# Softmax row sums by VectorE block transposes, with the sums' last merge taken from GpSimd, in an attention and mixture-of-experts layer

## What is computed

```python
h = _layernorm(x) * (1 + ca) + sa
xq, xk, xv = h @ wq.T, h @ wk.T, h @ wv.T        # each reshaped to (heads, 2048, 64)
scores = softmax(einsum('bhid,bhjd->bhij', xq, xk) * SCALE, axis=-1)
out = einsum('bhij,bhjd->bhid', scores, xv)
x = x + ga * (out.reshape(bsz, seqlen, 1024) @ wo.T)
h = _layernorm(x) * (1 + cb) + sb
x = x + gb * ffn(h)                              # routed experts and a shared one
```

## Time and profile before

| | |
|---|---|
| median of 3 runs | 1318.63 us (1318.17 to 1810.67) |
| the profiled execution | 1317.36 us |
| its span, first to last instruction | 1315.6 us |
| PE busy | 1297.5 us, 99% of the span |
| POOL busy | 1176.0 us, 89% |
| DVE busy | 911.3 us, 69% |
| ACT busy | 888.3 us, 68% |
| mean granted TensorE clock | 0.999 of full speed |

### The profile page before, as it was taken

How to read it: one execution, slowest core, us unless ns; L and a number is a source line. 1 busy time by engine, 2 the same in 40 slices (tenths; PEclk the granted TensorE clock), 3 DMA queues, 4 the chain that set the end, 5 groups by cost and what they waited for, 6 DMA issues and landing times. The chain is left out here.

```text
span 1315.6 us, 22284 instructions
## 1 busy us (share of the span) xinstructions
PE 1297.5 (99%) x8792; PEld 705.3 (54%) x8792; DVE 911.3 (69%) x1036; ACT 888.3 (68%) x1096; POOL 1176.0 (89%) x538
## 2 busy tenths in 40 slices
PE   7999999999999999999999999999999999999998
PEld 5545545454555545454555555454545545454787
DVE  6767667676767677677767676776767676859575
ACT  6666767676766766666766666676767667775474
POOL 2499999999999999999999999999999999999644
PEclk9999999999999999999999999999999999999999
DMA  8010202020110202020100202020200102001323
GB/s 210 11 39 1 49 1 49 1 49 1 27 24 1 49 1 49 1 49 1 38 13 1 49 1 49 2 49 0 49 1 10 40 1 49 1 1 30 101 73 89
DMA packets 31962, 41.55 MB, mean 32 GB/s; under 512 B 4298, under 2 KB 15186, under 8 KB 31858
## 3 DMA queue, kind: packets, MB, share of 16 engines
q1 hardware_dynamic: 31714, 40.13, 12.5%
q10 hardware_dynamic: 144, 0.00, 0.0%
HBM read 13.70 MB, written 1.11 MB: 11 GB/s over the span
## 5 line engine op out<-in xcount | busy, mean ns | idle before, releaser
L918 ACT ACTIVATE probs<-ps 128x1024 f32<-128x1024 f32 x512 | 498.7, 1032 | 78.7 <-PE ps L1348 75.9
L1079 DVE TENSOR_REDUCE peak_parts<-ps 128x2 f32<-128x1024 f32 x297 | 362.2, 1223 | 236.8 <-PE ps L1289 235.1
L1366 PE MATMUL ps<-probs,v_sb 128*64 128x512 f32 x2048 | 522.8, 606 | 0.0
L1009 POOL TENSOR_TENSOR acc<-acc,probs 128x1024 f32<-128x1024 f32 x192 | 457.7, 2384 | 31.2 <-ACT probs L918 29.6
L1009 POOL TENSOR_TENSOR acc_odd<-acc_odd,probs 128x1024 f32<-128x1024 f32 x192 | 459.5, 2393 | 0.0
L860 ACT COPY peak_copy<-ps 128x1024 f32<-128x1024 f32 x215 | 218.6, 1017 | 242.0 <-PE ps L1289 168.0
L1089 DVE TENSOR_REDUCE peak_parts<-peak_copy 128x2 f32<-128x1024 f32 x215 | 260.7, 1212 | 34.2 <-ACT peak_copy L860 34.2
L1366 PEld LDWEIGHTS ps<-probs,v_sb 128*64 128x64 f32 x2048 | 123.8, 136 | 157.3 <-issue 118.4
L1342 PE MATMUL ps<-q_hi,d_swap_hi 64*128 64x512 f32 x512 | 201.4, 393 | 0.4 <-ACT probs L918 0.4
L1342 PE MATMUL ps<-q_hi,d_hi 64*128 64x512 f32 x512 | 201.5, 394 | 0.0
L1348 PE MATMUL ps<-q_hi,d_swap_lo 64*128 64x512 f32 x512 | 200.7, 392 | 0.0
(11 more groups left out here) (237 smaller groups left out, 1571.6 us busy)
## 6 DMA issues: line engine op xcount, KB each, us to landing
k_swap_hi<-k_hi SPq DMA_DIRECT2D x64, 128.0 KB, 2.3
d_swap_hi<-d_hi SPq DMA_DIRECT2D x64, 128.0 KB, 2.3
d_swap_lo<-d_lo SPq DMA_DIRECT2D x64, 128.0 KB, 2.3
q_hi<-weights_dram SPq DMA_DIRECT2D x8, 256.0 KB, 3.2
q_lo<-weights_dram SPq DMA_DIRECT2D x8, 256.0 KB, 4.6
k_hi<-weights_dram SPq DMA_DIRECT2D x8, 256.0 KB, 5.9
k_swap_hi<-weights_dram SPq DMA_DIRECT2D x8, 256.0 KB, 5.3
probs<-in_L_ffn_w_dram SPq DMA_DIRECT2D x2, 512.0 KB, 5.9
```

Of the source, the lines that this page charges most:

```text
L918: act.activation(probs[:, kt % PROBS, :], ps[:, 2 * place:2 * place + 2, :].rearrange("p a b -> p (a b)"), ACT.Exp, scale=SCALE).then_inc( ...
L1009: pool.tensor_tensor(total, total, probs[:, kt % PROBS, :], ALU.add).then_inc(added, 1)
L1079: dve.tensor_reduce(peak_parts[:, :, i // STRETCHES, i % STRETCHES], ps[:, bank:bank + 2, :], AX.X, ALU.max).then_inc(peak_free, 1)
L1366: mm = pe.matmul(ps[at:at + HEAD_DIM, PV_BANK, :], v_sb[:, p, chunk_of(kt) * HEAD_DIM:(chunk_of(kt) + 1) * HEAD_DIM], probs[:, kt % PROBS, ...
```

## The change

The product with ones goes (but for the last unit), and POOL's merge with it (one merge is left, for the last unit), so that POOL makes 14 additions a unit; `acc_odd` is now double, one per half. In each unit, DVE makes the sums of the unit before: at place 4 it transposes `acc` in blocks of 32 x 32 into `k_raw` ("turn sum" 0), at place 6 it adds up each block's rows ("add sum" 0), at places 8 and 10 the same for `acc_odd`, turned into `acc`, and at place 12 it folds the partial sums ("fold": one 128x64 transpose, four 32x32 reductions, one more, and a reciprocal of 32x32). SP then writes the 1024 inverses to DRAM and, when they have landed, reads them back spread over 64 partitions each, in two DMAs. At place 20 (28 in the last unit) DVE multiplies `o_raw` with them. The output projection moves from place 22 of `half` 0 to place 14 of `half` 1. ACT's copy of k into `k_raw` waits for "add sum" 0, ACT's copy of `o_raw` and PE's projection wait for the multiplication of an earlier unit.

```diff
 LONG_JOBS = (
-    {2: ("q", 0), 6: ("sum", 0), 14: ("k", 0), 18: ("k", 1), 22: ("out", 0), 26: ("shift", 0)},
-    {2: ("q", 1), 6: ("v", 0), 10: ("sum", 0), 19: ("v", 1), 26: ("shift", 0)},
+    {2: ("q", 0), 14: ("k", 0), 18: ("k", 1), 26: ("shift", 0)},
+    {2: ("q", 1), 6: ("v", 0), 14: ("out", 0), 19: ("v", 1), 26: ("shift", 0)},
 )
...
+SUM_PLACES = {4: ("turn sum", 0), 6: ("add sum", 0), 8: ("turn sum", 1), 10: ("add sum", 1), 12: ("fold", 0)}
+SCALE_PLACE, LATE_SCALE_PLACE = 20, 28
...
-        acc_odd = sb("acc_odd", [P, HALF])
+        acc_odd = sb("acc_odd", [P, 2, HALF])
+        sum_parts = sb("sum_parts", [P, 64])
...
-        ADDS = TILES - 1
+        ADDS = TILES - 2
...
+            def spread_sums(unit_done):
+
+                parts = SumParts(unit_done)
+                sp.wait_ge(sums_inverted, unit_done + 1)
+                row = sums_dram[unit_done % 2:unit_done % 2 + 1, :]
+                sp.dma_start(row.rearrange("a (j i) -> (a j) i", j=32), parts.inverse).then_inc(sums_out, 16)
+                sp.wait_ge(sums_out, 16 * (unit_done + 1))
+                for b in range(2):
+                    sp.dma_start(parts.spread[b * HEAD_DIM:(b + 1) * HEAD_DIM, :],
+                                 row[:, b * BANK:(b + 1) * BANK].broadcast_to([HEAD_DIM, BANK])).then_inc(sums_spread, 16)
...
                     if kind == "k":
+                        if sums_before:
+                            act.wait_ge(sums_added, sums_before)
                         act.copy(k_raw[:, P + i * BANK:P + (i + 1) * BANK], job.ps).then_inc(raw_ready, 1)
...
-            def copy_pv(unit_done, sum_before):
+            def copy_pv(unit_done):
                 act.wait_ge(pv_done, PAIRS * unit_done)
-                if sum_before is not None:
-
-                    act.wait_ge(job_free, sum_before)
+                if unit_done > 1:
+                    act.wait_ge(out_scaled, unit_done - 1)
...
+            def turn_sum(unit_done, half_done, odd):
+
+                dve.wait_ge(added, unit_done * ADDS + (ADDS - 1 + odd))
+                dve.transpose(SumParts(unit_done).turned[odd], (acc_odd if odd else acc)[:, half_done, :]).then_inc(sums_turned, 1)
+
+            def add_sum(unit_done, odd):
...
+                dve.tensor_reduce(sum_parts[:, odd * 32:odd * 32 + 32],
+                                  parts.turned[odd].rearrange("p (j r) -> p j r", r=32), AX.X,
+                                  ALU.add).then_inc(sums_added, 1)
+
+            def fold_sums(unit_done):
...
+                link(dve.transpose(parts.parts_turned, sum_parts[:, :]))
+                for g in range(4):
+                    ins = dve.tensor_reduce(
+                        parts.quarters[:, g, :],
+                        parts.parts_turned[32 * g:32 * g + 32, :].rearrange("p (a i) -> p i a", a=2), AX.X, ALU.add)
+                link(ins)
+                link(dve.tensor_reduce(parts.sums, parts.quarters.rearrange("p g i -> p i g"), AX.X, ALU.add))
+                dve.reciprocal(parts.inverse, parts.sums).then_inc(sums_inverted, 1)
+
+            def scale_unit(unit_done, half_done):
+
+                dve.wait_ge(sums_spread, 32 * (unit_done + 1))
+                dve.wait_ge(o_copied, unit_done + 1)
+                dve.tensor_tensor(oT[:, half_done, :], o_raw[:, :], SumParts(unit_done).spread,
+                                  ALU.mult).then_inc(out_scaled, 1)
```

More of the change, by code:

```diff
@@ L81, in chunk_of, with side_jobs @@
     return half * 8 + pair * 2 + odd
-def side_jobs(half, sums=True, project=True, pairs=True, early=True, last_head=False, before_last=False):
+def side_jobs(half, sums=True, outs=True, project=True, pairs=True, early=True, last_head=False, before_last=False):
     places = [[] for _ in range(4 * PAIRS)]
     for place, (kind, i) in LONG_JOBS[half].items():
-        if sums if kind in ("sum", "out") else pairs if kind == "shift" else project:
+        if outs if kind == "out" else pairs if kind == "shift" else project:
             places[place].append((kind, i))
@@ L104, in side_jobs @@
     if sums:
-        for place, job in SCALE_PLACES[half].items():
+        for place, job in SUM_PLACES.items():
             places[place].append(job)
+        places[LATE_SCALE_PLACE if last_head and half == 1 else SCALE_PLACE].append(("scale", 0))
     if before_last:
@@ L238, in jobs_at @@
         def jobs_at(t):
-            return PROLOGUE_JOBS if isinstance(t, int) and t == 0 else t * (2 * JOBS_PER_HEAD) + (PROLOGUE_JOBS - 1)
+            return t * (2 * JOBS_PER_HEAD) + PROLOGUE_JOBS
         class Job:
@@ L278, in units @@
                     final_head = last and p == 1
-                    plan = side_jobs(half, sums=not (first and p == 0 and half == 0), project=not final_head,
+                    plan = side_jobs(half, sums=not (first and p == 0 and half == 0), outs=not (first and p == 0),
+                                     project=not final_head,
                                      pairs=not (final_head and half == 1), early=not final_head,
@@ L307, in build, with __init__ @@
         TAIL_PAIRED = 7
+        sums_dram = nc.dram_tensor("sums_dram", [2, HALF], F32, kind="Internal").ap()
+        class SumParts:
+            def __init__(self, unit_done):
+                even, odd = acc[:, unit_done % 2, :], acc_odd[:, unit_done % 2, :]
+                self.turned = [k_raw[:, P:P + HALF], even]
+                self.spread = odd[:, 0:BANK]
+                self.parts_turned = odd[:, BANK:BANK + 64]
+                self.quarters = odd[0:32, BANK + 128:BANK + 256].rearrange("p (g i) -> p g i", g=4)
+                self.sums = odd[0:32, BANK + 256:BANK + 288]
+                self.inverse = odd[0:32, BANK + 288:BANK + 320]
         def tail(kind, i):
@@ L781, in body @@
                             for kind, i in jobs:
+                                if kind == "fold":
+                                    spread_sums(unit - 1)
                                 if kind == "k":
@@ L831, in _, with side @@
                 keep_setup(n)
-            def side(job, kind, i, parity):
+            def side(job, kind, i, parity, sums_before=0):
                 cols = slice(i * BANK, (i + 1) * BANK)
@@ L923, in body @@
                                 if kind in COUNTED:
-                                    side(Job(jobs_at(t) + local), kind, i, 1 - p)
+                                    side(Job(jobs_at(t) + local), kind, i, 1 - p, max(0, 2 * unit - 1))
                                 if kind == "step k":
@@ L945, in body @@
                         if step == 0 and not first:
-                            copy_pv(unit, sums[-1] if sums else None)
+                            copy_pv(unit)
             pairs_of_heads(body)
-            copy_pv(UNITS, sums[-1])
+            copy_pv(UNITS)
             ffn_act(act)
@@ L988, in add @@
             def add(unit, half, n):
-                even, odd = acc[:, half, :], acc_odd[:, :]
+                even, odd = acc[:, half, :], acc_odd[:, half, :]
                 total = even if n % 2 == 1 else odd
-                if n == ADDS:
+                if n > ADDS:
                     pool.wait_ge(added, unit * ADDS + (n - 1))
@@ L1016, in _ @@
             pairs_of_heads(body)
+            add(UNITS - 1, 1, ADDS + 1)
             ffn_pool(pool)
@@ L1162, in body @@
                                     low_k(Job(jobs_at(t) + (local - 1)), i, 1 - p, head * 2 + (3 + i))
-                                if kind == "inv":
-                                    invert(i, Job(jobs_at(t) + (local - 1)))
+                                if kind == "turn sum":
+                                    turn_sum(unit - 1, 1 - half, i)
+                                if kind == "add sum":
+                                    add_sum(unit - 1, i)
+                                if kind == "fold":
+                                    fold_sums(unit - 1)
                                 if kind == "scale":
-                                    scale_outputs(Job(jobs_at(t) + (local - 1)), unit, 1 - half)
+                                    scale_unit(unit - 1, 1 - half)
                                 if kind == "out":
@@ L1453, in body @@
                                     pair(i, (unit + 2) * PEAK_PAIRS + i, head + 1, 1 - p, half, PEAK_BANK)
-                                if kind == "sum":
-                                    sum_unit(job, unit - 1, 1 - half)
                                 if kind == "out":
```

26 lines of the change are left out of this document (13 added, 13 removed).

## The result

The changed kernel takes 1332.2 us (median of 4 runs, 1330.1 to 1333.1) against 1319.0 for the kernel before, run beside it on the same chip: ratio 1.010, 95% interval 1.008 to 1.012; one of the four runs of the kernel before took 1810.67 us, and the ratio leaves it out. The forecast was 1327 us, +0.6%, "within 2%"; the range held it. The product with ones is gone, 26.6 us of TensorE work, and the kernel is 13 us slower.

A forecast was written before the change was run, and what follows sets the result against it. PE was taken to bound attention. 1317.36 (profiled) - 26.6 for the product + 32.2 for half 0 waits and scaling + 3 for odd units = 1326, with the median 1327 us (+0.6%); range 1302 to 1358.

The forecast's parts named there:

- The 0.86 of the product is all that the change can give.: On PE, 31 of 32 products with ones go, 0.86 us each: 26.6 us, 2.0% of the time, and nothing more.
- A transpose takes 1.22 us, between 0.69 and 2.4.: DVE's 1024-element transposes, shown in no row; rival of 2.3 us each gives 1372 us, chance 0.08.
- The fold takes 1.83 us.: DVE's fold of the partial sums, with transpose, additions, reciprocal and waits: 1.83 us, at least 1.5 if the four overlap.
- Half 0 carried forward: Place-by-place starts in a half 0 unit: DVE's lateness gives PE 2.05 us of new waits, at pairs 9, 10, 12, 15, 0.
- the sums' work: DVE's transposes, additions and fold in half 0: pairs 9, 10 and 12 come 0.1, 0.5 and 0.5 us late.
- pair 0's lateness: In half 0, behind the scaling and pair 15's late reduction, pair 0 comes at 5.11 for 4.57: 0.54 us.
- The scaling costs 0.25 us over 0.69 in half 0.: DVE's scaling at place 20 waits for POOL's addition in flight: 0.25 us more than 0.69, other end 2.3.
- The rival of whole additions: The scaling meets a whole POOL addition: 2.3 us instead of 0.25 in each half 0, 1356 us; chance 0.12.
- Half 1 has no wait, 36.8 us.: Half 1 units: v job, projection and idle time cover DVE's work; 35.87 - 0.86 + 1.75 (projection) = 36.8 us.
- The way through DRAM is hidden.: Store and spread of the inverses take 5 us, landing at about 22, before place 20; late-spread rival 1341 us, chance 0.05.
- +3 for the odd ones: An estimated 3 us added to the sum for the irregular units 1, 29 and 30.
- The room suffices: Rival: DVE's idle time absorbs the work, with shorter transposes or fold, so waits shrink; 1294 to 1314 us, chance 0.2.

The follow-up runs named there:

- e10: Changed kernel with DVE's sums work and scaling at other places, the last unit keeping the change's places, and SP's order mended: 1301.05 us, ratio 0.9875.
- e1: Changed kernel without the long transposes, long additions and the fold's sums on DVE; reciprocal, way through DRAM and scaling stay: 1311.35 us, ratio 0.9954.
- e2: Changed kernel with only the scaling moved, from place 20 to place 28: 1318.99 us, ratio 1.0013.
- e3: Changed kernel with the sums' transposes, long additions and fold sums left out and the scaling moved to place 28: 1297.97 us, ratio 0.9866.
- e4: Changed kernel with the output projection alone back at place 22 of half 0: 1345.23 us, ratio 1.0208.
- e8: Changed kernel with second transpose and addition, split fold and scaling at later places: 1309.74 us; with SP's order mended too, 1305.65 us.
- e5: Changed kernel with SP sending the last pass's row sums behind the first store of the routing weights: 1327.84 us, ratio 1.0072.

## Why the prediction was right, and where it was not

- **"The 0.86 of the product is all that the change can give."** Right. e10 gets 17.5 of the 26.6 us; most of the rest is the 0.56 us by which each of the 14 half 0 units exceeds 35.04, 7.8 us.
- **A transpose takes 1.22 us, between 0.69 and 2.4.** It takes 1.235 (31 of each in the profile). This choice carried the forecast; at 2.3 us it would have been 1372.
- **The fold takes 1.83 us.** From 726.11 to 728.04 it took 1.93: transpose 0.25 for 0.22, four additions 0.88 as forecast, the strided addition of 128 elements 0.37 for 0.28.
- **Half 0 carried forward.** Forecast starts, from the unit's start, against measured: pair 9 12.88, 12.90; pair 10 15.11, 15.11; pair 12 20.4, 20.40; pair 14 25.2, 25.28; pair 0 30.3 (30.55 with the scaling's 0.25), 30.57. Unit 37.3, 37.33. e1, e2 and e3 show three causes apart, against the forecast's terms: the sums' work 0.97 us (0.1 + 0.5 + 0.5), the scaling 0.79 (0.64 + 0.25), and pair 0's lateness 0.43 (0.54), which the forecast carried on behind the scaling and which stays without it.
- **The scaling costs 0.25 us over 0.69 in half 0.** It took 0.88, ending 0.55 us after POOL's addition. POOL in order of time, after, at the scaling of 737.24:

```profile
735.16 2.41 POOL L1034 TENSOR_TENSOR acc_odd<-acc_odd,probs 128x1024 f32<-128x1024 f32 x1
737.61 2.74 POOL L1034 TENSOR_TENSOR acc<-acc,probs 128x1024 f32<-128x1024 f32 x1
```

  POOL's next addition took 2.74 instead of 2.4: each side holds up the other. The rival of whole additions came true in one place, unit 29. DVE there, order of time:

```profile
1144.02 2.21 DVE L1170 TENSOR_TENSOR oT<-o_raw,acc_odd 128x512 f32<-128x512 f32 x1
...
1147.34 1.20 DVE L1105 TENSOR_REDUCE peak_parts<-ps 128x2 f32<-128x1024 f32 x1
```

  With the layer norm's statistics around it one more pair than in the earlier trace rows had to wait. The unit grew by 2.4 us: 0.9 as every half 1 unit did, and 1.0 by the scaling's place (e2, which moves it, has 38.84 us for 39.82); the last 0.5 I did not trace. PE there:

```profile
1148.59 0.50 PE L1352 MATMUL ps<-k_swap_hi,q_hi 64*128 64x512 f32 x2 [1.42 <-DVE peak_parts L1105]
```

- **Half 1 has no wait, 36.8 us.** 36.73, for the reason given: e4 takes the covering projection away and the waits appear.
- **The way through DRAM is hidden.** DVE waited for it once, 1.1 us, in the last unit; the two spreads landed in 3.0 us. What was missed is the other half of the same step: I named the copies of k as what stands behind SP's wait, and not the routing weights' store of the last unit, behind which ACT stood with its exponentials. Worth 2.5 us.
- **The term that was mis-sized is "+3 for the odd ones".** The regular units add 7.4 us by their measured lengths and 7.2 by the forecast's (14 x -0.35 and 13 x +0.93). Of the forecast's +8.6 that leaves 1.4 for everything else, which measured 6.9 in the profiled execution: units 1, 29 and 30 together +1.3, the end +3.7, unit 0 and what lies ahead of it +1.9. The last goes with the clock: 45 to 50 us after the start TensorE was granted half its clock in this execution. The window's rows, first before and then after:

```profile
45.00:50.00 5.00, 4.49 (x42) 3.14 (x44) 3.79 (x5) 2.60 (x4) 1.01 (x1) 1.00 0.02 4
```

```profile
45.00:50.00 5.00, 4.82 (x22) 3.43 (x24) 2.53 (x4) 1.60 (x2) 0.00 (x0) 0.50 0.01 4
```

  The granted clock is again the last column but two. Unit 0 took 34.6 us in the profiled executions of the kernel before, e1, e2, e3, e8 (both) and e10, all at full clock there. It took 35.7 in e5 and 35.8 in e4, where this window has 0.66, and 36.24 here with 0.50. So its length goes with the clock. Executions of one kernel differ in it: the 13 runs of the kernel before beside e1 to e4 had mean clocks from 0.996 to 1.000 and took 1319.3 to 1316.5 us. Whether the changed kernel also makes the stretch likelier stays open.
- **"The room suffices"** as a rival (1294 to 1314) was wrong for the change as written and right for its work: e8 to e10 fall there, with transposes of 1.23 us and a fold of 1.93, so not for the rival's reason of shorter instructions but by other places.

## What to carry to other kernels

Work moved from the bounding engine to one with idle time is worth its price only at the places where that idle time is: carry each place forward against the next thing that the bounding engine needs, and where it does not fit, move or split the new work before giving it up. Then look at the first and the last pass, where other jobs share the same places, and at every queue the new transfers join: ask not only whether they are late, but what now stands behind them. And a job of the bounding engine that happens to cover a late helper must be counted with what it covers: the projection hid 1.34 us at its new place and 0.43 at its old one.

## What the runs showed of the hardware

**A block transpose costs what a reduction does.** Groups by form, after:

```profile
L1143 DVE STREAM_TRANSPOSE k_raw<-acc 128x1024 f32<-128x1024 f32 x31 | 38.3, 1235 | 0.0
L1149 DVE TENSOR_REDUCE sum_parts<-k_raw 128x32 f32<-128x1024 f32 x31 | 37.5, 1209 | 0.0
L1159 DVE TENSOR_REDUCE acc_odd<-acc_odd 32x32 f32<-32x64 f32 x124 | 26.0, 210 | 2.4
L1170 DVE TENSOR_TENSOR oT<-o_raw,acc_odd 128x512 f32<-128x512 f32 x31 | 30.7, 990 | 1.1 <-DMA acc_odd<-sums_dram 1.1
```

An instruction on 32 partitions with 64 elements takes 0.21 us and four in a row 0.88: on four different quarters of the partitions they follow one another and do not overlap.

**DVE can be held up by more than one of POOL's additions.** This I had not expected; the forecast's upper end was one addition, 2.3 us. In e3's profiled execution one scaling took 10.51 us. DVE there:

```profile
109.64 10.51 DVE L1161 TENSOR_TENSOR oT<-o_raw,acc_odd 128x512 f32<-128x512 f32 x1
```

and POOL beside it:

```profile
107.96 2.38 POOL L1034 TENSOR_TENSOR acc_odd<-acc_odd,probs 128x1024 f32<-128x1024 f32 x1
110.28 2.41 POOL L1034 TENSOR_TENSOR acc<-acc,probs 128x1024 f32<-128x1024 f32 x1
112.65 2.35 POOL L1034 TENSOR_TENSOR acc_odd<-acc_odd,probs 128x1024 f32<-128x1024 f32 x1
114.96 2.34 POOL L1034 TENSOR_TENSOR acc<-acc,probs 128x1024 f32<-128x1024 f32 x1
117.25 2.34 POOL L1034 TENSOR_TENSOR acc_odd<-acc_odd,probs 128x1024 f32<-128x1024 f32 x1
```

The scaling began during one addition and ended 0.56 us after the fourth one behind it, when POOL had no tile left to add: PE had run dry behind the pair that DVE had not reduced. Unit 1 took 42.60 us (35.11 in e1) and unit 2 38.13 for 35.60. PE had stood still for 7.17 us, and from 117 to 127 us its mean granted clock was 0.51, so a part of this loss is the clock. That execution took 1307.1 us and the other three of the same kernel 1297.8 to 1298.0. It came back in e8 (10.95 us) and e10 at the scaling in unit 30. DVE in e10, and then the same instruction in e8 with SP's order mended:

```profile
1159.60 10.96 DVE L1176 TENSOR_TENSOR oT<-o_raw,acc_odd 128x512 f32<-128x512 f32 x1
```

```profile
1159.67 1.62 DVE L1174 TENSOR_TENSOR oT<-o_raw,acc_odd 128x512 f32<-128x512 f32 x1
```

Both began 1.3 us into an addition of POOL (1158.30 and 1158.39). In the second, POOL's next addition took 2.84 us instead of 2.4, so DVE got in at the first boundary; in the first it got in only after four more additions. In all profiles together 3 of 155 scalings at place 28 were held up for so long, and none of 124 at place 20; in the changed kernel itself the longest took 2.21 us. What decides at a boundary stays open, and I did not measure it by itself. In unit 30 the long scaling did not hold PE up: no pairs follow in unit 31, and its fifth tile's scores start 12.46 us into the unit in e10 and 12.45 in the run with the short scaling. The Trainium skill (SBUF — State Buffer, "Who interferes with whom") says that a VectorE instruction with two SBUF inputs contends with a GpSimd one that reads SBUF, and that the order of issue decides who blocks. The trace agrees for one addition; that a run of back-to-back additions can keep VectorE out for 10 us is more than the page says. Such an instruction belongs where POOL pauses, or gets one operand from PSUM, as the kernel before had it (L1112, 0.69 us on average over 32).
